# Lane weights of two edge sums: masks of six steps on VectorE, scaling on ScalarE

## The reference, cut to what matters

```python
deg = jax.ops.segment_sum(edge_weight, dst, num_segments=N)
agg = jax.ops.segment_sum(norm[:, None] * h[src], dst, num_segments=N)
```

## Time and profile before

| | |
|---|---|
| three runs | 10294.4, 10313.21, 10319.73 us; median 10313.21 |
| profiled execution | 10290.12 us, its span 10288.5 us |
| TensorE busy | 7709.8 us (75%) |
| VectorE busy | 6424.3 us (62%) |
| ScalarE busy | 1704.8 us (17%) |
| GpSimd busy | 6261.3 us (61%) |
| mean granted TensorE clock | 0.831 of full speed |
| degree stage | 140 to 690 us |
| first sum (sum_layer0) | 893 to 3240 us |
| second sum (sum_layer1) | 6362 to 9205 us |

### The profile page before, as it was taken

One profiled execution on the slowest core, in us unless ns is written; L12 is line 12 of the kernel. 1 busy time (PEld: TensorE's weight loads), 2 busy tenths in 40 slices (PEclk: granted clock), 3 DMA queues, 4 the chain that ended last, 5 costly groups with the idle time before them and its releaser, 6 DMA issues. The chain is left out here.

```text
span 10288.5 us, 140782 instructions
## 1 busy us (share of the span) xinstructions
PE 7709.8 (75%) x33473; PEld 5537.9 (54%) x33473; DVE 6424.3 (62%) x21734; ACT 1704.8 (17%) x3275; POOL 6261.3 (61%) x6430
## 2 busy tenths in 40 slices
PE   4643666667666888888888885887887788777779
PEld 3432555555554666666666663555555555545557
DVE  6874777777776555555555554666666666657752
ACT  0000000000000333343343331110011001002210
POOL 2233777777775877777777775666666666640002
PEclk7556888888887888888888886888888888879989
DMA  1015333333332111111111112333333333323335
GB/s 47 24 33 140 108 106 108 108 108 106 108 107 85 15 17 16 15 17 16 16 17 15 17 15 58 93 92 95 90 93 92 92 93 94 93 75 95 95 88 168
DMA packets 463651, 738.90 MB, mean 72 GB/s; under 512 B 144891, under 2 KB 317083, under 8 KB 462663
## 3 DMA queue, kind: packets, MB, share of 16 engines
q0 software_dynamic: 235408, 494.89, 18.7%
q1 hardware_dynamic: 214540, 224.57, 7.7%
q10 hardware_dynamic: 13240, 15.44, 0.5%
HBM read 624.19 MB, written 108.44 MB: 71 GB/s over the span
## 5 line engine op out<-in xcount | busy, mean ns | idle before, releaser
L897 POOL DMA_INDIRECT sum_gathered<-table,sum_idx x3600 | 3499.5, 972 | 1250.8 <-issue 1008.5
L962 PE MATMUL sum_agg_res<-sum_gathered,sum_lay 125*125 125x256 f32 x7200 | 2294.8, 459 | 1084.3 <-DVE all_sums L947 406.5
L1468 POOL DMA_INDIRECT sorted_recs<-fin_rec,fin_pos x1700 | 2115.6, 1244 | 502.8 <-issue 499.4
L962 PEld LDWEIGHTS sum_agg_res<-sum_gathered,sum_lay 125*125 125x125 f32 x7200 | 1489.3, 221 | 1715.8 <-DVE all_sums L947 1213.1
L947 DVE TENSOR_TENSOR all_sums<-all_sums,sum_agg_res 125x256 f32 x3600 | 1512.5, 420 | 1051.1 <-PE sum_agg_res L962 885.1
L928 DVE TENSOR_SCALAR sum_lay<-all_lane,sum_dloc_now,sum_w_now 125x125 f32<-125x125 f32 x3612 | 1293.5, 358 | 20.8 <-DVE sum_xn_tiles L1079 17.0
L1899 PE MATMUL fin_ps_up<-fin_tokens_T,fin_w 128*128 128x250 f32 x3200 | 988.9, 445 | 0.0
L1907 PE MATMUL fin_ps_dn<-fin_w,fin_hidden 128*125 128x256 f32 x3200 | 859.8, 404 | 10.3 <-DVE fin_acc L1537 10.3
L1899 PEld LDWEIGHTS fin_ps_up<-fin_tokens_T,fin_w 128*128 128x128 f32 x3200 | 692.0, 230 | 165.5 <-issue 65.6
L1537 DVE SCALAR_TENSOR_TENSOR fin_acc<-fin_ps_dn,fin_comb,fin_acc 125x256 f32<-125x256 f32 x800 | 383.5, 482 | 574.3 <-PE fin_ps_dn L1907 562.4
L1907 PEld LDWEIGHTS fin_ps_dn<-fin_w,fin_hidden 128*125 128x125 f32 x3200 | 600.3, 197 | 127.5 <-issue 49.4
(11 more groups left out here) (479 smaller groups left out, 10956.6 us busy)
## 6 DMA issues: line engine op xcount, KB each, us to landing
sum_gathered<-table,sum_idx POOLq DMA_INDIRECT x3600
sorted_recs<-fin_rec,fin_pos POOLq DMA_INDIRECT x1700
slice_weights<-slices_sw SPq DMA_DIRECT2D x50, 480.0 KB
out_sw<-slice_weights SPq DMA_DIRECT2D x50, 480.0 KB
deg_x_tiles<-in_x SPq DMA_DIRECT2D x100, 125.0 KB
sum_x_tiles<-in_x SPq DMA_DIRECT2D x100, 125.0 KB
fin_x<-in_x SPq DMA_DIRECT2D x100, 125.0 KB
x<-fin_acc SPq DMA_DIRECT2D x100, 125.0 KB
```

Of the source, the lines that this page charges most:

```text
L897: eng.indirect_dma_start(out=self.rows[:, s % self.RING, :], out_offset=None, in_=self.table, in_offset=bass.IndirectOffsetOnAxis(ap=self. ...
L962: eng.matmul(self.res[s % self.RES][:, 0, :], self.lay[:, g % 2, l, :], self.rows[0:P, s % self.RING, :], start=True, stop=True).then_inc( ...
L1468: eng.indirect_dma_start(out=k.sorted_recs, out_offset=bass.IndirectOffsetOnAxis(ap=pos[:, n, r:r + 1], axis=0), in_=rec[:, n, r, :], in_o ...
```

## The change

VectorE no longer builds weighted matrices. Once for six steps it compares lane numbers, held six times over (k.lanes, bf16), with the six places of each edge (dloc_p, now bf16), into a bf16 mask of 125 x 125 x 6 with the step innermost (find). ScalarE multiplies each step's mask by its weight into the fp32 matrix (build, now an activation with a per-partition scale), and copies the weights of an iteration (take_weights). ScalarE's programs of both sums are cut into the same 24 half groups, with the builds of a half group behind its other work. Two tile copies of the places go. The degree stage's one-hots are made six at once in the same way, with the step innermost, so that TensorE loads them with a stride of six elements. The tile of key maxima is allocated in another place. Arithmetic, gathers and adds stay.

```diff
             eng.memset(ones[:], 1.0).then_inc(ones_done, 1)
+            if layer == 0:
+                link(eng.tensor_copy(k.lanes[:, :, :], k.lane[0:P, :].unsqueeze(2).to_broadcast([P, 128, GRP])))
...
-        dl = sb("dloc_now", [P, STEPS])
-        hot = sb("hot", [P, 2, GRP, 128], BF16)
+        hot = sb("hot", [P, 2, 128, GRP], BF16)
...
                 eng.wait_ge(deg_done, i * GRPS + g + 1)
-                for l in range(GRP):
-                    ins = eng.tensor_scalar(hot[:, g % 2, l, :], lane16[:], dl[:, g * GRP + l:g * GRP + l + 1], None,
-                                            ALU.is_equal)
-                ins.then_inc(hot_ready, 1)
+                steps = k.dloc_p[:, bass.ds(i * STEPS + g * GRP, GRP)]
+                eng.tensor_tensor(hot[:, g % 2, :, :], k.lanes[:, :, :], steps.unsqueeze(1).to_broadcast([P, 128, GRP]),
+                                  ALU.is_equal).then_inc(hot_ready, 1)
...
-                eng.tensor_copy(dl[:], k.dloc_p[:, bass.ds(i * STEPS, STEPS)]).then_inc(dl_ready, 1)
...
-                    mm = eng.matmul(ps_deg[half][:, at + l, :], hot[:, g % 2, l, :], ws[:, g * GRP + l, :],
+                    mm = eng.matmul(ps_deg[half][:, at + l, :], hot[:, g % 2, :, l], ws[:, g * GRP + l, :],
...
+        self.mask = sb("mask", [P, 2, P, GRP], BF16)
         self.lay = sb("lay", [P, 2, GRP, P])
-        self.dl = sb("dloc_now", [P, STEPS + GRP])
...
-    def take_local(self, i, turn, first=False):
+    def find(self, i, g):
         eng, k = self.nc.vector, self.k
-        if not first:
-
-            eng.wait_ge(self.lay_ready, i * GRPS + 1)
-        eng.tensor_copy(self.dl[:], k.dloc_p[:, bass.ds(i * STEPS, STEPS + GRP)]).then_inc(self.local_ready, 1)
-        eng.tensor_copy(self.wl[:], k.w_p[:, bass.ds(i * STEPS, STEPS + GRP)]).then_inc(self.local_ready, 1)
-        eng.wait_ge(self.local_ready, turn * 2 + 2)
+        eng.wait_ge(self.lay_ready, i * GRPS + g)
+        steps = k.dloc_p[:, bass.ds(i * STEPS + g * GRP, GRP)]
+        eng.tensor_tensor(self.mask[:, g % 2, :, :], k.lanes[:, 0:P, :], steps.unsqueeze(1).to_broadcast([P, P, GRP]),
+                          ALU.is_equal).then_inc(self.masked, 1)
+
+    def scalar_start(self):
+        self.nc.scalar.sem_inc(self.lay_ready, 1)
+
+    def take_weights(self, i, turn):
+
+        eng, k = self.nc.scalar, self.k
+        eng.wait_ge(self.lay_ready, i * GRPS + 1 + turn)
+        eng.copy(self.wl[:], k.w_p[:, bass.ds(i * STEPS, STEPS + GRP)]).then_inc(self.local_ready, 1)
+        eng.wait_ge(self.local_ready, i + 1 + turn)
     def build(self, i, g, l):
-        eng, k = self.nc.vector, self.k
+        eng = self.nc.scalar
         s = g * GRP + l
         if l == 0:
+            eng.wait_ge(self.masked, i * GRPS + g + 1)
             eng.wait_ge(self.multiplied, i * STEPS + g * GRP + self.RING - GRP)
-        ins = eng.tensor_scalar(self.lay[:, g % 2, l, :], k.lane[0:P, 0:P], self.dl[:, s:s + 1], self.wl[:, s:s + 1],
-                                ALU.is_equal, ALU.mult)
+        ins = eng.activation(self.lay[:, g % 2, l, :], self.mask[:, g % 2, :, l], ACT.Copy, scale=self.wl[:, s:s + 1])
         if l == GRP - 1:
             ins.then_inc(self.lay_ready, 1)
...
-            eng.wait_ge(self.lay_ready, i * GRPS + g + 1)
+            eng.wait_ge(self.lay_ready, i * GRPS + g + 2)
...
-            agg.take_local(0, 0, first=True)
-            for l in range(GRP):
-                agg.build(0, 0, l)
+            agg.find(0, 0)
             with eng.Fori(0, k.NSUP) as i:
-                agg.take_local(i, i + 1)
                 source_hots(i, 0)
                 for h, batches in enumerate(spans(NB4)):
                     g = h // 2
...
+                    if h % 2 == 0:
+                        agg.find(i, g + 1)
                     for l in range(h % 2 * GRP // 2, (h % 2 + 1) * GRP // 2):
-                        agg.build(i, g + 1, l)
                         agg.add(i, g, l)
...
+            agg.scalar_start()
+            agg.take_weights(0, 0)
+            for l in range(GRP):
+                agg.build(0, 0, l)
             with eng.Fori(0, k.NSUP) as i:
-                for j in range(TS):
+                agg.take_weights(i, 1)
+                for h in range(2 * GRPS):
+                    j, part = divmod(h, 6)
                     t = i * TS + j
-                    eng.wait_ge(T_done, t + 1)
-                    eng.wait_ge(k_done, t + 1)
-                    eng.copy(xnT[:, :, :], ps_T[:, :, :]).then_inc(xnT_ready, 1)
-                    eng.wait_ge(kd_ready, t + 2)
-                    eng.wait_ge(ctx_done, t + TS)
-                    eng.activation(ek[:], kd[:], ACT.Exp).then_inc(ek_ready, 1)
+                    if part == 1:
+                        eng.wait_ge(T_done, t + 1)
+                        eng.wait_ge(k_done, t + 1)
+                        eng.copy(xnT[:, :, :], ps_T[:, :, :]).then_inc(xnT_ready, 1)
+                    elif part == 4:
+                        eng.wait_ge(kd_ready, t + 2)
+                        eng.wait_ge(ctx_done, t + TS)
+                        eng.activation(ek[:], kd[:], ACT.Exp).then_inc(ek_ready, 1)
+                    for l in range(h % 2 * GRP // 2, (h % 2 + 1) * GRP // 2):
+                        agg.build(i, h // 2 + 1, l)
...
             def run(i):
-                agg.take_local(i, i + 1)
                 for h in range(2 * GRPS):
+                    if h % 2 == 0:
+                        agg.find(i, h // 2 + 1)
                     for l in range(h % 2 * GRP // 2, (h % 2 + 1) * GRP // 2):
-                        agg.build(i, h // 2 + 1, l)
                         agg.add(i, h // 2, l)
...
+            def run(i):
+                agg.take_weights(i, 1)
+                for h in range(2 * GRPS):
+                    if h == 0:
+                        keep_T1(i)
+                    elif h == 1:
+                        keep_queries(i, 0)
+                    elif h == 2:
+                        exp_low(i, 0)
+                        keep_queries(i, 1)
+                        exp_low(i, 1)
+                    elif h == 14:
+                        keep_T2(i)
+                    elif 15 <= h < 15 + NF:
+                        keep_hidden(i, h - 15)
+                    for l in range(h % 2 * GRP // 2, (h % 2 + 1) * GRP // 2):
+                        agg.build(i, h // 2 + 1, l)
...
+        k.lanes = sb("lanes", [P, 128, GRP], BF16)
...
-    k.dloc_p = sb("dloc_p", [P, k.NS + GRP])
+    k.dloc_p = sb("dloc_p", [P, k.NS + GRP], BF16)
```

More of the change, by code:

```diff
@@ L2288, in _, with keep_T1 @@
             eng.wait_ge(S.consts, 2)
-            def run(i):
+            agg.scalar_start()
+            agg.take_weights(0, 0)
+            for l in range(GRP):
+                agg.build(0, 0, l)
+            def keep_T1(i):
                 for c in range(2):
@@ L2314, in run, with keep_hidden @@
                     eng.copy(xT[:, c, :], ps_A[c][:, 0:T]).then_inc(S.T2_kept, 1)
[L2315 to L2320 removed]
+            def keep_hidden(i, u):
+                eng.wait_ge(S.up_done, i * NF + u + 1)
+                after(eng, S.dn_done, i * (NF + 1) + u)
+                eng.activation(hid[:, u % 2, :], ps_C[u % 2][:, 0:T], ACT.Relu, bias=b1[:, u:u + 1])\
+                   .then_inc(S.up_kept, 1)
+            def run(i):
[15 more added lines that the diff above has]
+                        agg.build(i, h // 2 + 1, l)
             supertiles(eng, run)
```

34 lines of the change are left out of this document (13 added, 21 removed).

## The result

| | before | after |
|---|---|---|
| median | 10314.7 us | 10413.9 us |
| ratio (95% interval) | | 1.0101 (1.0083 to 1.0118) |
| profiled execution | 10290.1 us | 10408.1 us |
| from the first gather to the last, first sum | 2333.3 us | 2329.7 us |
| the same, second sum | 2831.1 us | 3053.5 us |

The change made the kernel 1.0% slower, 99 us. The forecast was 25 us slower, 10338: the sign is right and the size is 76 us short, inside the stated range. A second comparison beside the experiments gave 1.0124 (1.0107 to 1.0141). In the profiled executions the difference is 118 us: the degree stage and its head of the first sum gave 112 back, the first sum 4, the second sum took 222, and 12 lie in stages that the change doesn't touch (3121.6 us between the sums became 3131.5; it was 3120.5 in a second profile of the same kernel, so this part is scatter between executions).

The account below looks back on a forecast made before the run. Bounds: VectorE in the degree stage, GpSimd's gathers in the first sum, the hand-over chain (front) and TensorE (back) in the second. -100 + 25 + 100 = +25 us on the median 10313 gave 10338 us, range 10235 to 10465.

Parts of the forecast that it names:

- The degree stage, -100 us: Degree stage: joint one-hots and a shorter head, middle and tail save 4.1 us in each of 25 iterations.
- The bound from strided weight loads: Degree stage: lower bound of the saving, 25 us, if 12-byte-strided weight loads lose their overlap or one-hots take 0.95 us.
- The mask at 0.56 us: Both sums, VectorE: a mask of 750 elements takes 0.56 us, at twice the rate of the comparisons in the trace.
- the rival of one element a cycle: Masks take 0.93 us and one-hots 0.95, in all +140 us, 10453 us; chance 0.15.
- The first sum, +25 us: First sum, bound by GpSimd's gathers: 300 masks each add 86 ns of gather time; bounds 0 and 150 us.
- The rival in which each mask holds up a gather: First sum: each mask delays a gather by 0.5 us, +150 us, 10463 us; chance 0.08.
- The second sum, +100 us: Second sum: scalings queued behind ScalarE's other work delay TensorE by 3.95 us in each of 25 iterations; bounds 0 and +170.
- h = 16: Second sum, after the first feed-forward product: TensorE waits 2.1 us an iteration for scalings queued behind ScalarE's keep.
- h = 18: Second sum, with h = 20 and 22: weights come 0.36 us late each time, 1.1 us an iteration for the three.
- from h = 4 VectorE is late rather than TensorE: Second sum's front: VectorE is the late one from h = 4, leaving +0.75 us an iteration, bounds -1 and +3.
- Rival 1: VectorE's builds did bound the second sum, which then costs 15 us instead of 100: 10253 us; chance 0.30.
- Table switches: Rival: ScalarE's scalings switch its function table some 20 times an iteration of the second sum, over 600 us; chance 0.03.

Follow-up runs that it names:

- The back alone: Changed kernel with the second sum's scalings ahead of the keeps only in half groups h < 14, behind them in the back: 0.9993, second sum 2928.2 us.
- all ahead: Changed kernel with each half group's three scalings in the second sum moved ahead of ScalarE's keep: 10183.9 us, 0.9903, second sum 2839.0 us.
- The front alone: Changed kernel with the second sum's scalings ahead of the keeps only from h = 14 on, behind them in the front: 0.9972, second sum 2905.3 us.
- With the gaps filled: Unused TensorE products in the second sum's gaps: changed kernel 10222 us (sum 2865.2), against builds on VectorE, rest as changed, 10118 us (sum 2767.8).
- with fillers: Changed kernel with scalings ahead of the keeps, plus unused TensorE products in the second sum's gaps: 10098 us, 0.9797, second sum 2752.0 us.
- the builds on VectorE: Slower chip: changed degree stage with both sums as before, 0.9917; changed kernel with only the second sum's builds back on VectorE, 0.9903.
- degree-stage run: Kernel before with only the degree stage's new one-hots, both sums as before: 0.9917 on a chip where the kernel before takes 11402 us.

## Why the prediction was right or wrong

- **The degree stage, -100 us: right.** 24 iterations go from 21.28 us (the prediction calls them 22) to 16.98 each, 25 x 4.3 = 107 us. The one-hots take 554 ns where I had 0.57 us. The bound from strided weight loads was real: it costs some 28 us and is inside that number.
- **The mask at 0.56 us: right** (546 ns), so the rival of one element a cycle is out. Add to add stayed at 0.65 us (starts at 7609.72, 7610.37, 7611.02), with 0.42 us of add and 0.23 of turn-round, so the builds had indeed cost nothing there.
- **The first sum, +25 us: the size was wrong, the bound of zero was met.** Gathers went from 1739.5 us to 1743.7, and to 1738.6 in the second profile, so the growth is scatter. 84 of the 300 masks lie beside a gather of over 980 ns (79 in the second profile), but the number of such gathers went from 176 to 169 and 142, so others vanished elsewhere. The step that failed took one comparison's share of lengthened gathers (86 ns) for a price of each. Why the total doesn't grow with the masks wasn't tried; that they take over a part of what other operations stretched before is a guess. The rival in which each mask holds up a gather falls with it.
- **The second sum, +100 us: the mechanism and the places were right, the sum was not.** Of the three places, h = 16 and h = 18 came out at 1.97 and 0.35 us against 2.1 and 0.36, in part by luck: three scalings take 1.15 us where I had 0.96, and 0.12 and 0.23 us pass from their end to the multiply where I had 0.25. With h = 20 and 22 the waits of the back are 2.8 us an iteration against 3.2. The back alone costs 89 us (80 forecast), but that agreement is luck too, as 4.8 us more of its back are at half clock than with all ahead (12.3 against 7.5) and the forecast had idle time only. The front alone costs 66 (19 forecast): the step that failed is the sentence that from h = 4 VectorE is late rather than TensorE. Group 2's first three scalings are queued behind the second query's keeps and its exponential, so all six start at 7624.22, and TensorE waits 2.73 us at h = 4 just as it does at h = 2. I had followed the queue for one slot and not for the next.
- **The clock, which had no term.** I had read that the back runs at full clock and took that as given. It changed with the gaps. With the gaps filled the loss is 97 us, with the clock as it falls 222. That 97 is close to the forecast's 100 is no proof of its terms: it lies to about equal parts in the front (2.2 us an iteration, some 55 us, where I had 19) and in the back (the same, where I had 80), and it is a lower bound. The miss of the total is here and in the front's second wait (+122 us on the second sum's term), less what the first sum (29) and the degree stage (7 to 12) came out better.
- **Rival 1, builds did bound the second sum: half true.** The 266 us of waits ended by a build were nearly all replaced by other waits: with the scalings out of the way the second sum is 2839.0 us against 2831.1. VectorE's relief shortens the front (62.2 to 59.9 us) and the back takes it back (51.1 to 54.0, with 7.5 us at half clock in place of 1.6). Only with the clock up is it worth something, 2752 against 2768.
- **Table switches: none,** as forecast.
- **What beats both:** the degree stage as changed and the scalings ahead of the keeps, 0.9903; with fillers 0.9797. Without fillers all of that gain is the degree stage's (107 us by its iterations, where the whole kernel gains 105; the second sum is 8 us longer than before), so to move the builds to ScalarE brought nothing by itself: on the slower chip the builds on VectorE gave 0.9917 and 0.9903 and the scalings ahead 0.9893, with intervals that overlap.

## What to carry to other kernels

When work moves to another engine's queue, its length is the smaller question. Write down, for each place where it lands, what that queue waits for just ahead of it, and whether the one who needs the result is the one that ends that wait; if so, put the work ahead of the wait. And where TensorE bounds a stretch at full clock, ask what each new gap does to the clock behind it. Here the half speed cost up to as much again as the idle time; the granted clock of the stretch is a part of the forecast, not a constant.

## What the runs showed of the hardware

- **Filling TensorE's gaps keeps its clock up.** With 27 unused products an iteration in the version with the scalings ahead, the clock of the front goes from 0.73 to 0.92 in the iterations shown (30.5 to 8.9 us at half clock by the means) and the kernel gets 86 us faster (10184 to 10098 us), though TensorE does more. The Trainium skill ("TensorE: Matmul & The Clock Gate", section "HAM oscillation — how this bites in real kernels") says that idle gaps bring the slow clock back, and the trace agrees; that filling them pays although the results are thrown away is shown here by the three runs with fillers.
- **A stride of six bf16 elements, 12 bytes, isn't free.** It costs ScalarE 63 ns on 125 elements (388 to 451) and TensorE's weight load of 128 columns 39 ns (102 to 141). The Trainium skill ("ScalarE: Activation LUTs", section "What ACT_TABLE_LOAD costs") gives an activation with a pointer operand 280 ns and 0.833 ns an element, an estimate of 384 ns; the trace agrees without the stride and not with it. The Trainium skill ("SBUF — State Buffer", section "Door 1: The DMA port swizzle") also says that a read which crosses to another 16-byte line pays, with which this agrees, and that bf16 may stride by 8 elements for free; there the measurement decides against it.
- **A comparison of bf16 tensors took 0.5 ns an element beyond a fixed part taken as 167 ns** where six neighbours lie side by side in both inputs and in the result (750 elements in 546 ns), and at 1.02 where one element is repeated along the inner run.
- **Two chips differ by 10% on the same kernel.** The kernel before takes 10289 to 10315 us in four of the five comparisons and 11402 in the other. The gathers are as long (949 ns by the median there), but the engines idle where the profile names nothing that they wait for. Waits of the degree-stage run there, in the first sum:

```profile
ACT sum_exp_key L1110 <- issue: 600.4, 48, 17.5
...
PE sum_agg_res L958 <- issue: 322.1, 161, 8.7
```

Neither row has a counterpart in the first sum of the kernel before on the first chip. The expectations call this a stall for instructions, and the traces don't bear that out. In this sum TensorE, ScalarE and VectorE have 280 such gaps of over 1 us, while 149 packets of 8 KB arrive on the queue that brings instructions, and only 25 of the gaps end 1.2 to 1.9 us after a packet; in the kernel before 48 of 72 such gaps do, all of them VectorE's. What the engines wait for there stays open. It is a reason to compare only kernels that ran on the same chip, or on chips where the kernel before takes the same time.
